# One DMA for each replicated load of a scan kernel, and the first expert weights issued earlier

## The reference

```python
xn = layernorm(x)
# scan: N = 32 states for each of 256 channels
dt = softplus(xn @ dt_w.T + dt_b); A = -exp(log_A)
b, c = xn @ B_w.T + B_b, xn @ C_w.T + C_b
h = exp(A * dt_t) * h + (dt_t * x_t) * b_t      # for each t, channel, state
y_t = sum_n(h * c_t) + D_skip * x_t
# experts: 8 of them, top 2 of softmax(xn @ wg), capacity 2*T/8 tokens each
out_e = relu(tokens_e @ w1[e] + b1[e]) @ w2[e] + b2[e]
x = x + y + gated sum of each token's two experts
```

## Time and profile before

| | us |
|---|---|
| median of 3 runs | 4012.66 |
| lowest, highest | 4011.36, 4013.64 |
| profiled execution | 4012.38 |
| its span, first to last instruction | 4010.7 |

### The profile page before, as it was taken

One profiled execution on the slowest core, in us unless ns is written; L12 is line 12 of the kernel. 1 busy time (PEld: TensorE's weight loads), 2 busy tenths in 40 slices (PEclk: granted clock), 3 DMA queues, 4 the chain that ended last, 5 costly groups with the idle time before them and its releaser, 6 DMA issues.

```text
span 4010.7 us, 70861 instructions
## 1 busy us (share of the span) xinstructions
PE 3328.8 (83%) x16548; PEld 2166.8 (54%) x16548; DVE 3699.5 (92%) x2500; ACT 2529.3 (63%) x4779; POOL 3252.5 (81%) x1722
## 2 busy tenths in 40 slices
PE   7697788888887888888887888878887888888887
PEld 4375555555555555555555555555555555555554
DVE  6797999989999999999998999989999999999997
ACT  3213666766666667666666667667666667666665
POOL 0004989888888989888898999889888999888886
PEclk9898999999999999999999999999999999999998
DMA  9954666565666656575666656575667656575666
GB/s 326 342 75 117 158 152 154 137 164 150 161 151 171 156 147 146 138 177 151 157 159 167 159 146 148 138 173 157 160 154 172 156 142 148 138 178 149 158 160 155
DMA packets 382792, 646.23 MB, mean 161 GB/s; under 512 B 86717, under 2 KB 258881, under 8 KB 382081
## 3 DMA queue, kind: packets, MB, share of 16 engines
q1 hardware_dynamic: 289458, 539.05, 48.6%
q0 software_dynamic: 67776, 85.24, 13.8%
q10 hardware_dynamic: 25104, 16.91, 1.9%
HBM read 515.68 MB, written 142.80 MB: 164 GB/s over the span
## 4 chain that ended last, share of the span: by engine, by line
issue 27%; POOL 26%; PE 12%; SPq 11%; DVE 8%; DMA 7%; ACT 6%; POOLq 1%; ACTq 1%; DVEq 0%
POOL u L1003 16%; SPq L331 7%; PE bank L627 5%; POOL out_rows L962 5%; DMA dt<-dt_rows 3%; DVE h L1194 3%; PE bank L574 3%; POOL xg L950 3%; DVE hc L1183 3%; SPq L319 3%; ACT bank L775 2%; DMA dt<-x 2%; DMA w_sb<-w 2%; ACT ht L817 1%; PE bank L534 1%
## 5 line engine op out<-in xcount | busy, mean ns | idle before, releaser
L1003 POOL TENSOR_TENSOR u<-dtx,b_sb 128x1024 f32<-128x1024 f32 x1024 | 2492.4, 2494 | 232.9 <-DVE h L1194 203.8
L1194 DVE TENSOR_TENSOR_SCAN h<-bank,u 128x1024 f32<-128x1024 f32 x1024 | 2302.3, 2277 | 44.0 <-ACT bank L775 30.6
L775 ACT ACTIVATE bank<-dt,a_neg 128x1024 f32<-128x1024 f32 x1026 | 1129.0, 1108 | 548.7 <-DMA dt<-dt_rows 247.3
L627 PE MATMUL bank<-xgt,w_sb 128*128 128x256 f32 x4096 | 1088.2, 412 | 349.9 <-ACT ht L817 163.6
L1183 DVE TENSOR_TENSOR hc<-h,bank 128x2048 f32<-128x2048 f32 x514 | 1165.0, 2267 | 175.8 <-ACT bank L845 175.2
L627 PEld LDWEIGHTS bank<-xgt,w_sb 128*128 128x128 f32 x4096 | 782.1, 201 | 746.4 <-issue 650.7
L636 PE MATMUL bank<-w_sb,ht 128*128 128x256 f32 x4096 | 938.8, 382 | 49.5 <-ACT o_sb L832 32.3
L636 PEld LDWEIGHTS bank<-w_sb,ht 128*128 128x128 f32 x4096 | 762.4, 190 | 244.6 <-issue 149.2
L817 ACT ACTIVATE ht<-bank,b_sb 128x256 f32<-128x256 f32 x1024 | 424.0, 464 | 313.6 <-PE bank L627 279.4
L586 PE MATMUL bank<-hc,rsum 128*32 128x512 f32 x4112 | 552.7, 610 | 4.2 <-DVE hc L1183 4.2
L962 POOL DMA_INDIRECT out_rows<-o_sb,sidx x258 | 415.6, 1611 | 124.8 <-issue 65.0
(11 more groups left out here) (105 smaller groups left out, 1866.9 us busy)
## 6 DMA issues: line engine op xcount, KB each, us to landing
b_sb<-bc_rows SPq DMA_DIRECT2D x1032, 128.0 KB
c_sb<-bc_rows SPq DMA_DIRECT2D x1032, 128.0 KB
dt<-dt_rows SPq DMA_DIRECT2D x528, 128.0 KB, 4.4
dtx<-dtx_rows SPq DMA_DIRECT2D x528, 128.0 KB, 2.8
w_sb<-w SPq DMA_DIRECT2D x18, 1024.0 KB, 9.8
dt_rows<-dt_n SPq DMA_DIRECT2D x137, 128.0 KB, 3.1
dtx_rows<-dtx_n SPq DMA_DIRECT2D x137, 128.0 KB
out_rows<-y_sb POOLq DMA_DIRECT2D x34, 512.0 KB
```

The costliest lines, as they stand in the source:

```text
L627: mm = pe.matmul(m_ps[:, c, :], w1_sb[:, kk, ch * P:(ch + 1) * P], xgt[:, kk, :], start=(kk == 0), stop=(kk == KD - 1))
L775: act.activation(a_ps[k % 2], dt[:, k % GPP, :], ACT.Exp, scale=a_neg[:, col:col + 1]).then_inc(a_ready, 1)
L1003: pool.tensor_tensor(u[:, k % UB, :], dtx[:, gp, :], b_sb[:, j, :], ALU.mult).then_inc(u_ready, 1)
L1194: dve.tensor_tensor_scan(h[:, k, :], a_ps[k % 2], u[:, k % UB, :], 0.0, ALU.mult, ALU.add).then_inc(scan_done, 1)
```

## The change

Two things. First, `load_bc` and `load_group` issue one DMA of 128 partitions where they issued four of 32; the source's pattern repeats its rows by a step of zero. The semaphores then get 16 for a load, and all waits count so. Second, at the last step of an expert the load of `w1`, with its two waits, stands ahead of `next_dt(1)` and `next_dt(2)` rather than behind them.

```diff
             def load_bc(dst, sem_in, row, jj):
 
                 first = jj // (2 * NG) % 4 * 2 * N + row + jj % NG * R
-                for r in range(R):
-                    src = bc_d[bass.ds(first + r, 1), :].rearrange("a t -> (a t)").partition_broadcast(RD)
-                    sp.dma_start(dst[r * RD:(r + 1) * RD, :], src).then_inc(sem_in, 16)
+                src = bc_d[bass.ds(first, R), :].unsqueeze(1).to_broadcast([R, RD, S])
+                sp.dma_start(dst, src).then_inc(sem_in, 16)
...
                 src = src_d[(par * NQ + gh * GPP + gp) * RD:(par * NQ + gh * GPP + gp + 1) * RD, :]
-                for r in range(R):
-                    sp.dma_start(dst[r * RD:(r + 1) * RD, gp, :], src).then_inc(sem_in, 16)
+                sp.dma_start(dst[:, gp, :], src.partition_broadcast(R)).then_inc(sem_in, 16)
...
                     next_b(1)
-                    if last:
-                        next_dt(1)
-                        next_dt(2)
                     if s == SPE - 1:
                         sp.wait_ge(fill_done, st * FS + FD)
                         settle(sp)
                         sp.wait_ge(w1_in, 16 * (e + 1))
                         settle(sp)
                         load_w1((e + 1) % E)
+                    if last:
+                        next_dt(1)
+                        next_dt(2)
                     next_c(0)
...
-                            pool.wait_ge(dtx_in[gp], 16 * R * (hf + 1))
+                            pool.wait_ge(dtx_in[gp], 16 * (hf + 1))
```

More of the change, by code:

```diff
@@ L472, in _ @@
             for i in range(2):
-                sp.wait_ge(b_in[i], 16 * R * (STEPS + 1))
-                sp.wait_ge(c_in[i], 16 * R * (STEPS + 1))
+                sp.wait_ge(b_in[i], 16 * (STEPS + 1))
+                sp.wait_ge(c_in[i], 16 * (STEPS + 1))
             for gp in range(GPP):
-                sp.wait_ge(dt_in[gp], 16 * R * (2 * B + 1))
-                sp.wait_ge(dtx_in[gp], 16 * R * (2 * B + 1))
+                sp.wait_ge(dt_in[gp], 16 * (2 * B + 1))
+                sp.wait_ge(dtx_in[gp], 16 * (2 * B + 1))
             sp.wait_ge(b_st, 16 * (NG + 2 + STEPS) + 1)
@@ L793, in _ @@
             for k in range(2):
-                act.wait_ge(dt_in[k], 16 * R)
+                act.wait_ge(dt_in[k], 16)
                 decay(k, k)
             slots_in(1)
-            act.wait_ge(c_in[1], 16 * R)
+            act.wait_ge(c_in[1], 16)
             act.activation(c_ps, c_sb[:, 1, 0:HALF], ACT.Copy).then_inc(c_ready, 1)
@@ L837, in c_copy @@
                         if i == 0:
-                            act.wait_ge(c_in[1], 16 * R * (st + 2))
+                            act.wait_ge(c_in[1], 16 * (st + 2))
                             act.wait_ge(dt_done, p + 2)
@@ L841, in c_copy @@
                             if i == 2:
-                                act.wait_ge(c_in[0], 16 * R * (st + 1))
+                                act.wait_ge(c_in[0], 16 * (st + 1))
                             act.wait_ge(hc_done, 4 * st + i + 1)
@@ L878, in _ @@
                         if tng == 0 and tk < GPP:
-                            act.wait_ge(dt_in[tk], 16 * R * (2 * b + ts // HPB + 1))
+                            act.wait_ge(dt_in[tk], 16 * (2 * b + ts // HPB + 1))
                         act.wait_ge(scan_done, st * NG + k + 1 + SCAN0)
@@ L998, in _ @@
                         if gp == 0:
-                            pool.wait_ge(b_in[j], 16 * R * (st + 1))
+                            pool.wait_ge(b_in[j], 16 * (st + 1))
                         if ng == 0 and k < GPP:
-                            pool.wait_ge(dtx_in[gp], 16 * R * (hf + 1))
+                            pool.wait_ge(dtx_in[gp], 16 * (hf + 1))
                         pool.wait_ge(scan_done, st * NG + k - UB + 1 + SCAN0)
```

## The result

The changed kernel takes 5176.34 us (median; 5174.15 to 5183.52) where the kernel before, timed beside it, takes 4013.15 us: 1.29 times as long, 95% interval 1.2878 to 1.2922. The forecast had the sign, and that each merged load runs on four engines. The time lies in its range of 5150 to 8550 us, near the low end. But 7150 us, the likeliest, was too high by 1974 us: +3137 us were forecast and +1163 us came. The time is that of rival 1, 5250 us.

A forecast was written before the change was run, and what follows sets the result against it. Computing bounded the kernel before, with loads costing a few us per half; afterwards four DMA queues would. 355 us before `u`, 5916 loads, 798 other traffic and 80 hand-overs gave 7149, said as 7150 us; range 5150 to 8550 us.

The forecast's parts named there:

- rival 1: Replicated loads on four engines at the fast rate, 25.8 GB/s each; ordinary steps stay hidden, 5250 us; chance 20%.
- Four engines a load: Each merged load, with 4 outermost in its source, is dealt to the same four engines, 102.2 MB each.
- at the queue's mean of 17.3 GB/s: 5916 us: Time four engines need for the replicated loads at SyncE's queue's mean rate over all shapes; the rate chosen.
- The fast end: Upper engine rate for the replicated loads, 25.8 GB/s from a lone `xnt` load; they would need 3963 us.
- 355 + 3857 + 798 + 80: Forecast's sum with its 5916 us replaced: start until `u`, replicated loads, other traffic, queues running dry in 32 halves.
- the 90 that the prediction gave as a sign: Whole-kernel DMA rate expected after the change: about 90 GB/s, with bytes staying at 646 MB.
- The slow end, 14.1 GB/s: Lower engine rate, from late in a `b` load at 225 GB/s over 16 engines; loads would need 7271 us.
- Rival 2: Replicated loads on four engines at the slow rate, 14.1 GB/s each: 8500 us; chance 23%.
- The other traffic, 798 us: Loop's stores, gathers, scatters and weights, spread over 16 engines: 798 us per engine, also on the four.
- The last step: Last step of a half, with twelve replicated loads where ordinary steps have four; forecast needed 97 us.
- The rival with 16 engines: Merged loads still dealt to 16 engines, only issuing cheaper and weight waits possibly gone: 3830 us; chance 11%.
- SyncE late nowhere: Sign expected after the change: SyncE waits less for `u` and is itself late nowhere.

The follow-up runs named there:

- experiments 2 and 3: Against the changed kernel, other partition orders or DMA counts: 16 engines on 128 partitions 3853.1 us, on 64 3997.49 us; eight engines 4313.69 us; two 8846.24 us.
- inter2x16: Against the changed kernel: partition order channel * 4 + state, two DMAs of 64 partitions a load, outermost count 16; 3997.49 us, ratio 0.9977 to before.
- merge16: Against the changed kernel: partition order channel * 4 + state, one DMA a load, source's outermost count 32; 3853.1 us, ratio 0.961 to before.
- experiment 1: Each part alone: merged loads with w1 where it was, 5175.17 us; early w1 on the kernel before, 4018.62 us against 4007.85 us.

## Why the prediction was right or wrong

- **Four engines a load: right.** The small packets count them, the share of 0.26 shows them, and experiments 2 and 3 turn them to 16, 8 and 2.
- **The rate of an engine: wrong, and this is the step that failed.** The sum took the term "at the queue's mean of 17.3 GB/s: 5916 us" for 102.2 MB an engine. Measured in the last step is 106 GB/s over four engines, 26.5 each, with which 102.2 MB take 3857 us. The difference, 2059 us, is more than the whole error of 1974: with it the same sum is 355 + 3857 + 798 + 80 = 5090 us, 86 below the measured time. The fast end, 25.8 GB/s from the `xnt` window, was the right row. For the same reason the mean fell to 125 GB/s only and not to the 90 that the prediction gave as a sign.
- **The reason given for the mean: wrong twice.** It was "the same queue's rate over mostly these very loads". First, a queue's mean holds other shapes as well: the changed kernel's own is 538.86 MB / (0.295 x 16 x 5174.6 us) = 22.1 GB/s, though its loads run at 26.5. Second, the loads themselves ran slower before, with 16 engines on DMAs of 32 partitions. A longer window of the `b` load of the earlier trace rows in the kernel before shows

```profile
1517.40:1518.90 1.50, 1.50 (x11) 0.31 (x9) 1.50 (x1) 1.50 (x2) 1.50 (x2) 1.00 0.86 265
```

That is 265 / (0.86 x 16) = 19.3 GB/s for a busy engine, like the loads of `inter2x16` on 64 partitions and unlike those of `merge16` on 128.

- **The slow end, 14.1 GB/s: misread.** It is 225 / 16 and leaves out the share of 0.87, by which the `xnt` rate had been divided; with it the row gives 16.2, and the window above 19.3. What the prediction saw in 225 GB/s, an agreement with a limit of eight ports, rests on a window of 1.02 us; the longer one has 265. Rival 2, built on the 14.1, did not happen: four engines at work together run at 26.5 each. Why they escape what `inter2x16` shows for 16 is open.
- **The other traffic, 798 us: of the right order, not measured by itself.** The loop of the changed kernel, first to last `u`, is

```profile
362.20:5098.70 4736.50, 3191.95 (x15162) 2081.10 (x15163) 3413.50 (x1658) 2428.49 (x4592) 3224.34 (x1695) 0.86 0.41 118
```

A share of 0.41 is 1942 us an engine. The loads at 26.5 GB/s, spread over 16, are 964 of it, so the prediction's own subtraction leaves 978 us here. The four engines then have 3857 + 798 = 4655 us of work by the one figure and 4835 by the other, in a loop of 4736.5 us. They are busy nearly throughout by this estimate, as forecast; only the work is less than the 6714 us of the sum.

- **Rival 1: right in its working.** It had 26.6 us for an ordinary step and 153 us a half; the windows show 28.7 and 25.9, and 146.9 for four steps, while the loop's mean is 148.0 a half. It had 5250 us, measured 5176. Its sign came too, though not in full: ScalarE waited for `c` once, 6.5 us, and GpSimd for `b` only 42 times.
- **The last step: right in kind.** 70 us until `dt(3)` is in, by rival 1; in the timeline SyncE starts at 1968.94, and ScalarE's decay that waited for the last `dt` starts at 2037.62.
- **w1: right for the change, wrong alone.** It is worth nothing in the changed kernel (experiment 1). Alone it was costed at a gain of 0 to 59 us and gave a loss of 11, of which the cause is open.
- **Issues: not told apart from the faster packets.** The rival with 16 engines had 3830 us from two rows, the last step's excess and the weight waits; `merge16` gives 3853, but it has faster packets as well as fewer issues. The DMA share of its last step is 0.86 of a shorter step, so the 95% before did not give the saving back.
- **SyncE late nowhere: wrong.** In the last step shown it stood 3 to 6 us in most of its later issues, and over the whole run 3.6 us in the median of `dt`'s. The chain has 12% + 7% of the span on its issues at L329 and L318, where the earlier trace rows had 7% + 3%.

## What to carry to other kernels

Merging replicated loads into one DMA paid here when the source's outermost count was 32, by 4%; with a count of 4 it cost 29%. Reordering the partitions raised it from 4 to 32, and the count of small packets for a DMA told the number of engines in one look. The runs tried counts of 2, 4, 8, 16 and 32 on the source, with 32 or more partitions on the destination; other counts are not shown. When a transfer is put on fewer engines, take an engine's rate from a window where those bytes alone are moving, divided by the share of busy engines, and not from a queue's mean, which holds other shapes and other layouts.

## What the runs showed of the hardware that was not expected

- A DMA engine moves about 26 GB/s of 4 KB packets, with four at work (106 GB/s, 26.5 each) as with two (52 GB/s for SyncE's queue, 26 each).
- SyncE's issuing instruction is held while the engines behind it are far behind: about 0.56 us for the same issue in an ordinary step, 3 to 6 us late in a last step of the changed kernel. These are two rows of the changed kernel, the whole run's loads by L329, min, median and max in ns:

```profile
L329 SPq DMA_DIRECT2D dt<-dt_rows x132: 554/3556/7070, 340.4 to 5140.4; - x132
L329 SPq DMA_DIRECT2D dtx<-dtx_rows x132: 553/2875/6746, 341.2 to 5106.5; - x132
```

- The same 16 engines are slower on a DMA of 64 partitions than on one of 128, 19.4 and 20.2 against 24.0 to 24.9 GB/s each, in loads of `inter2x16` and `merge16`. The Trainium skill, page "SBUF — State Buffer", section "Door 1: The DMA port swizzle", would have eight ports for 64 partitions and 16 for 128; the direction agrees, a full halving is not what the runs show.
